# One decoder kernel: in its last attention, four heads' products in four groups of rows together, and one output tile a batch

## The reference

```
def _L1_xattn_ref(q, k, v, Wq, bq, Wk, bk, Wv, bv, Wo, bo):
    qh = (q @ Wq + bq).reshape(B, LQ, HEADS, D_K).transpose(0, 2, 1, 3)
    kh = (k @ Wk + bk).reshape(B, LKV, HEADS, D_K).transpose(0, 2, 1, 3)
    vh = (v @ Wv + bv).reshape(B, LKV, HEADS, D_K).transpose(0, 2, 1, 3)
    scores = jnp.einsum('bhqd,bhkd->bhqk', qh, kh) * scale
    attn = jax.nn.softmax(scores, axis=-1)
    out = jnp.einsum('bhqk,bhkd->bhqd', attn, vh)
    concat = out.transpose(0, 2, 1, 3).reshape(B, LQ, D_MODEL)
    return concat @ Wo + bo
```

## Time and profile before

| | |
|---|---|
| median of 3 runs | 792.78 us (789.83 to 793.07) |
| profiled execution, its own time | 796.1 us |
| its span | 794.3 us |
| busy: TensorE, VectorE, ScalarE, GpSimd | 719.1, 489.1, 412.9, 290.0 us |
| mean granted clock of TensorE | 0.937 of 2.4 GHz |

### The profile page before, as it was taken

The page is one execution under the profiler, slowest core; times in us unless marked ns, Lnnn a source line. Parts: engine busy times, 40 slices in busy tenths (PEclk is TensorE's granted clock), DMA queues, the critical chain, the costliest instruction groups (busy, mean ns, idle before and its releaser), DMA issues.

```text
span 794.3 us, 16402 instructions
## 1 busy us (share of the span) xinstructions
PE 719.1 (91%) x5852; PEld 542.2 (68%) x5852; DVE 489.1 (62%) x1297; ACT 412.9 (52%) x1047; POOL 290.0 (37%) x395
## 2 busy tenths in 40 slices
PE   8788889898897998999999989989888899999886
PEld 6565567575665765899898967758566455767665
DVE  4669777887977885444543455545455658583643
ACT  2234556657566677554544467555562545454311
POOL 0015355565555666110000036423350646363300
PEclk8869989999999999999999999999998756999999
DMA  8537451533727471000000000001011501000000
GB/s 235 126 69 179 123 128 43 122 83 88 161 46 205 112 214 57 2 1 1 1 1 1 1 1 4 1 2 41 4 38 54 185 26 31 2 2 9 8 7 7
DMA packets 25175, 48.11 MB, mean 61 GB/s; under 512 B 7264, under 2 KB 14192, under 8 KB 25096
## 3 DMA queue, kind: packets, MB, share of 16 engines
q1 hardware_dynamic: 24376, 45.66, 22.7%
q10 hardware_dynamic: 720, 1.41, 0.5%
HBM read 17.49 MB, written 0.52 MB: 23 GB/s over the span
## 4 chain that ended last, share of the span: by engine, by line
PE 60%; DVE 14%; issue 10%; ACT 8%; SPq 3%; POOL 2%; DMA 2%; POOLq 0%; ACTq 0%; DVEq 0%
PE SC L839 7%; PE G L550 7%; PE SC L826 7%; PE SC L769 5%; PE G L625 4%; PE SC L861 3%; PE G L938 3%; DVE shift_cols L1542 3%; PE SO L812 3%; ACT causal_probs L1154 2%; PE SO L893 2%; PE SC L743 2%; PE G L647 2%; SPq L1769 1%; PE G L577 1%
## 5 line engine op out<-in xcount | busy, mean ns | idle before, releaser
L1169 ACT ACTIVATE exps<-SC 128x512 f32<-128x512 f32 x192 | 114.4, 597 | 106.8 <-PE SC L769 106.1
L1542 DVE TENSOR_REDUCE shift_cols<-SC 128x2 f32<-128x512 f32 x192 | 129.5, 684 | 32.0 <-PE SC L743 31.5
L1621 POOL TENSOR_TENSOR rstd<-variance,consts 128x2 f32<-128x2 f32 (+1 forms) x48 | 36.8, 766 | 266.0 <-DVE variance L1234 263.0
L1689 POOL TENSOR_TENSOR VB<-exps 128x256 f32<-128x256 f32 x128 | 95.7, 756 | 59.4 <-ACT exps L1169 58.6
L1143 ACT ACTIVATE hidden<-SC,cols 128x256 f32<-128x256 f32 x128 | 53.6, 471 | 65.4 <-PE SC L826 65.3
L1711 POOL TENSOR_TENSOR causal_probs<-causal_probs,inverse 128x256 f32<-128x256 f32 x64 | 51.6, 828 | 68.9 <-DVE inverse L1555 68.9
L1576 DVE SCALAR_TENSOR_TENSOR R<-SC,small,R 128x128 f32<-128x128 f32 x128 | 39.0, 346 | 54.0 <-PE SC L839 53.3
L1154 ACT ACTIVATE causal_probs<-SC,negmax 128x128 f32<-128x128 f32 (+1 forms) x128 | 52.3, 424 | 37.1 <-DVE negmax L1550 37.0
L769 PE MATMUL SC<-stacked_q,stacked_k 100*128 100x256 f32 x256 | 66.9, 344 | 3.5 <-DMA stacked_q<-shift_rows 1.9
L839 PEld LDWEIGHTS SC<-ffn_w,hidden 128*128 128x128 f32 x512 | 66.0, 192 | 5.3 <-issue 1.8
L839 PE MATMUL SC<-ffn_w,hidden 128*128 128x128 f32 x512 | 67.6, 276 | 0.0
(11 more groups left out here) (257 smaller groups left out, 1504.5 us busy)
## 6 DMA issues: line engine op xcount, KB each, us to landing
stacked_k<-k_hi SPq DMA_DIRECT2D x64, 128.0 KB, 2.4
stacked_q<-q_hi SPq DMA_DIRECT2D x64, 128.0 KB, 2.4
ffn_w<-in_ffn_w SPq DMA_DIRECT2D x16, 512.0 KB, 4.8
stacked_k<-k_lo SPq DMA_DIRECT2D x32, 128.0 KB, 2.4
stacked_q<-q_lo SPq DMA_DIRECT2D x32, 128.0 KB, 2.5
packed_k<-U SPq DMA_DIRECT2D x48, 32.0 KB, 1.9
packed_q<-YN SPq DMA_DIRECT2D x48, 32.0 KB, 1.9
a_weights<-in_a_li SPq DMA_DIRECT2D x3, 256.0 KB, 7.4
```

Source lines behind the costliest of these rows:

```text
L1169: fn(exps[:, n % EXPS, :, :].rearrange("p t q -> p (t q)"), SC[1][:, n % 2, :, :].rearrange("p t q -> p (t q)"), ACT.Exp, scale=ATTENTIONS ...
L1542: v.tensor_reduce(shift_cols[:, n // UNIT % 4, :, n % UNIT], SC[0][:, n % 2, :, :], axis=AX.X, op=ALU.max, negate=True).then_inc(head_max, 1)
L1689: v.tensor_tensor(kept[n % EXPS].rearrange("p t q -> p (t q)"), exps[:, n % EXPS, 0, :], exps[:, n % EXPS, 1, :], ALU.add).then_inc(kept_r ...
```

## The change

- The products of the cross attention get a function of their own, `cross_products`: every second slot, at the front, for heads n and n+1 and, with a lag of 10 slots (CROSS_LAG), for the transposed products of heads n-10 and n-9. The eight matmuls go to the four groups of rows and to four banks, in turn. It waits for `head_max` of all heads before n and for `head_exp` of all before n-10.
- All 16 heads of a batch go into one bank: outputs in columns 0 to T, sums in columns T to 2T. The values of unit u have their 8 columns moved by 8 u in the 32, among zeros (`clear_values`, two clearings on GpSimd; `cross_values` writes in two parts), and the ones for the sums likewise (`own_rows`). The four units accumulate.
- ScalarE draws the sums, GpSimd checks, VectorE refines and divides once a batch (18, 18, 19 and 19 slots behind the last unit's first head), when all outputs have been written. The first unit of the next batch waits for the division.
- `project_out` has one chunk in place of four; `lx_wo` is 128 x 128. `mix(b)` begins one slot later (slot 16 b + 32).

The core of the diff:

```diff
-SHIFT_LAG = 9
+SHIFT_LAG, CROSS_LAG = 9, 10
+CROSS_INVERT, CROSS_REFINE, CROSS_DIVIDE = 18, 19, 19
+CROSS_OUT_AFTER = HEADS - UNIT + CROSS_DIVIDE + 1
...
 def mix_at(b):
-    return LX_AT + HEADS * b + OUT_AFTER
+    return LX_AT + HEADS * b + CROSS_OUT_AFTER
...
 def project_out(s, t):
...
-                    if at["d"] == HD:
+                    if s // NB == LX:
+                        c0, chunks = 4 * (s % 2), 1
+                        pe.wait_ge(cross_divided, CROSS_UNIT + s % NB + 1)
...
+                def cross_products(n, m):
+                    if n is not None:
+                        if n == STACK_HEADS:
+                            pe.wait_ge(exp_ready, NB * PAIRS)
+                            pe.wait_ge(key_ones_in, 16 * 2)
+                        pe.wait_ge(head_max, n)
+                        if n % UNIT == 0:
+                            pe.wait_ge(packed_in[n // UNIT % 4], 16 * 6 * (stream_of(n) % NB + 1))
+                    if m is not None:
+                        pe.wait_ge(head_exp, m)
+                        if m % UNIT == 0:
+                            pe.wait_ge(shifts_in[m // UNIT % 4], 16 * (m // UNIT // 4 + 1))
+                    for t in range(TT):
+                        of = slice(t * P, (t + 1) * P)
+                        if n is not None:
+                            for h in (n, n + 1):
+                                q, kk = packed(h, HD - 1)
+                                last = mm(SC[0][:, h % 2, t, :], q[:, of], kk, start=True, stop=True)
+                                if t == TT - 1:
+                                    last.then_inc(shift_scores, 1)
+                        if m is not None:
+                            for h in (m, m + 1):
+                                q, kk = packed(h, HD)
+                                last = mm(SC[1][:, h % 2, t, :], kk[:, of], q, start=True, stop=True)
+                                if t == TT - 1:
+                                    last.then_inc(head_scores, 1)
...
+                def cross_sum(U_):
+                    n, u = UNIT * U_, U_ % 4
+                    if u == 0:
+                        cross_place(stream_of(n) % NB)
+                    pe.wait_ge(kept_ready, n + UNIT)
+                    own = const("own_rows")[:, HD0 * (3 - u):HD0 * (3 - u) + HD]
+                    for k in range(UNIT):
+                        mm(SO[HD * k:HD * k + HD, T:2 * T], own, kept[(n + k) % EXPS].rearrange("p t q -> p (t q)"),
+                           start=u == 0, stop=False)
+                def cross_place(b):
+                    if b == 0:
+                        wait_emptied(pe, ("OC", 4 * NB - 1))
+                    else:
+                        pe.wait_ge(cross_divided, CROSS_UNIT + b)
+                def cross_unit_values(U_):
...
+                            last = mm(SO[HD * k:HD * k + HD, 0:T], cross_value(s, kt, h0 + k), exps[:, (n + k) % EXPS, kt, :],
+                                      start=False, stop=u == 3 and kt == TT - 1)
+                    last.then_inc(cross_outputs, 1)
...
+                def cross_sums_drawn(b):
...
+                    act.wait_ge(cross_outputs, CROSS_UNIT + 4 * (b + 1))
+                    fn(unit_sums[:, b % 2, :], SO[:, T:2 * T], ACT.Copy)
+                    fn(unit_inverse[:, b % 2, :], SO[:, T:2 * T], ACT.Ln).then_inc(cross_drawn, 1)
```

More of the change, by code:

```diff
@@ L122 @@
 LX_AT = L1_AT + NB * PAIRS
-LAST = LX_AT + HEADS * (NB - 1) + OUT_AFTER + 31
+LAST = LX_AT + HEADS * (NB - 1) + CROSS_OUT_AFTER + 31
 LINEAR_SLOTS = [
@@ L187, in head_of, with late_head @@
     return None
+def late_head(slot, more=0):
+    for lag, last in ((SHIFT_LAG, False), (CROSS_LAG, True)):
+        n = head_of(slot - lag - more)
+        if n is not None and (n >= STACK_HEADS) == last:
+            return n
+    return None
 def unit_of(slot, at):
@@ L193, in unit_of, with stacked_unit, cross_batch @@
     return n // UNIT if n is not None and n % UNIT == 0 else None
+def stacked_unit(slot, at):
+    U_ = unit_of(slot, at)
+    return U_ if U_ is not None and U_ < CROSS_UNIT else None
+def cross_batch(slot, at):
+    U_ = unit_of(slot, at)
+    return (U_ - CROSS_UNIT) // 4 if U_ is not None and U_ >= CROSS_UNIT and U_ % 4 == 3 else None
 def stream_of(n):
@@ L419, in decoder @@
         hidden_ready = sem("hidden_ready")
+        cross_outputs, cross_divided, cross_drawn = bank_filled["out"][0], bank_emptied["out"][0], bank_emptied["pair"][0]
         tile_number, tiles_of = {}, {r: 0 for r in RINGS}
@@ L972, in front @@
                 def front(slot):
-                    if head_of(slot) is not None:
-                        head_products(head_of(slot))
+                    n, m = head_of(slot), late_head(slot)
+                    if n is not None and n < STACK_HEADS:
+                        head_products(n)
+                    even = [h if h is not None and h >= STACK_HEADS and h % 2 == 0 else None for h in (n, m)]
+                    if even != [None, None]:
+                        cross_products(*even)
                     if unit_of(slot, TURN_AT) is not None:
@@ L1472, in cross_values @@
                     g = wait_filled(dve, ("v", s))
-                    v.tensor_tensor(VB[s % 2][:, 0:TT * C].rearrange("p (t c) -> p t c", c=C),
-                                    g[:, 0:TT * C].rearrange("p (t c) -> p t c", c=C), over_tiles(row("bv")), ALU.add)\
-                        .then_inc(*emptied(("v", s)))
+                    dve.wait_ge(packed_cleared, 4 + s % 2 + 1)
+                    if b >= 2:
+                        dve.wait_ge(cross_outputs, CROSS_UNIT + 4 * (b - 1))
+                    for t in range(TT):
+                        part = [x.rearrange("p (u k d) -> p u k d", u=4, k=UNIT)
+                                for x in (g[:, t * C:(t + 1) * C], row("bv"))]
+                        last = v.tensor_tensor(cross_values_of(s, t), part[0], part[1], ALU.add)
+                    last.then_inc(*emptied(("v", s)))
                     yield 1
```

160 lines of the change are left out of this document (104 added, 56 removed).

## The result

The changed kernel takes **808.7 us** (median of 4 executions, 797.9 to 817.4) against 792.9 (4 executions, 789.8 to 795.0): ratio **1.0128, 95% interval 1.0067 to 1.0189**. It is slower; the forecast was 785 us, range 769 to 799. The interval leaves out executions more than 1.5% above the fastest of the same kernel, and here that cuts off the upper part of one continuous spread, so the median shows more than the ratio.

The account below looks back on a forecast made before the run. The last attention was taken as mostly TensorE-bound, with VectorE full from 700.8 to 711.4. Terms by stage summed to -8.8 us, giving 784.0 against the median of 792.8; forecast 785 us, range 769 to 799.

Parts of the forecast that it names:

- Products together: Cross attention: eight matmuls cost what four did, saving TensorE 0.43 us (full clock) or 0.73 (half) per pair of slots.
- rival 3: Whole kernel: gain and waits cancel, also if eight matmuls are not as cheap at full clock; 790 to 792 us; chance 0.20.
- light stage: First transposed product to batch 0's slot tables, 612.6 to 674.1, 38 slots: sum -3.2 us, taken as -3.
- What that adds: Each group waits for both maxima and exponentials of the last: bare pair 1.9 us at full clock, four slots 4.2.
- The pair with a turn: Cross attention, pair whose slots include the turn's matmul and ScalarE's copy: 2.3 us at full clock, 2.9 at half.
- 592.8 to 612.6: Causal layer's rest beside the first scores: nine single products become five groups, -1.7 us, taken as -1.5.
- The stretches with `up1`: 677.9 to 700.8 and 713.8 to 736.3: savings of 3.1 us each, cancelled by 3.1 of waits; nothing left.
- 700.8 to 711.4 and 736.3 to 743.8: VectorE-bound stretches: fewer refinements and divisions, -1.5 us in the first and -1.3 in the second.
- From 743.8 on: End of the kernel: batch 3's output products leave TensorE's chain, -1.5 us.
- The tile: One tile a batch: 12 of 16 refinements and divisions, 12 draws and checks, three quarters of output products removed; 1.35 us a batch.
- The clock: Least certain term, 612.6 to 674.1: all at half clock some 65 us (+3.7), at full about 50 (-12).
- The second: Rival: each of 37 groups waits for the later of VectorE and ScalarE; at 0.35 us extra each, 797 us; chance 0.23.

Follow-up runs that it names:

- tile_only: The kernel before with only the one tile a batch; products single as before, lag 9; 799.0 us, ratio 1.0052.
- again: The changed kernel, unaltered, run and profiled once more; 811.4 us, ratio 1.0122.
- early: The changed kernel with both exponentials and both maxima of a pair moved to the front of the group's slot; 795.8 us, ratio 1.002.
- exps_early: The changed kernel with only ScalarE's two exponentials of a pair moved to the front, maxima one a slot; 808.1 us, ratio 1.0158.
- early_tight: The changed kernel with both exponentials and maxima moved to the front, and each batch's draws, guess, refinement and division one slot earlier; 801.5 us, ratio 1.0019.
- before_again: The kernel before, unaltered, with a profile of its own; 795.2 us, ratio 0.9999.
- after_warm: The changed kernel with three unused matmuls of zeros ahead of each group's wait in slots 10 to 46; 804.2 us, ratio 1.0097.
- tile_warm: One tile a batch with single products, plus two matmuls of zeros before each head's products in slots 10 to 46; 827.4 us, ratio 1.0409.

## Why the prediction was wrong, step by step

- **Products together.** Right: eight in 0.44 us at full (679.17 to 679.61) and 0.74 at half clock (645.29 to 646.03). The remark under rival 3 that no row at full clock shows eight together overlooked one in the trace of before: 707.95 to 708.40. In the light stage TensorE's work fell by 14.9 us; the forecast had 12 + 2.7.
- **What that adds: the step that failed.** I put 2.7 and 2.9 us on a pair at half clock and 4.2 on two pairs at full clock, and some 4 us besides on the steps in between. The groups of after at full clock:

```profile
624.01 0.38 PE L796 MATMUL SC<-packed_k,packed_q 31*128 31x256 f32 x2
...
626.33 0.39 PE L796 MATMUL SC<-packed_k,packed_q 31*128 31x256 f32 x2 [0.94 <-ACT exps L1284]
...
629.18 0.39 PE L796 MATMUL SC<-packed_k,packed_q 31*128 31x256 f32 x2 [0.71 <-DMA packed_q<-shift_rows]
```

The pair with a turn (624.01 to 626.33) took the 2.3 us forecast; at half clock such pairs took 2.8 (617.93 to 620.76), forecast 2.9. What failed is the other pair. It took 2.9 us at full clock (626.33 to 629.18) where the sum has 1.9, and with the projections 5.6 and 7.1 us (612.34 to 617.93, 638.20 to 645.29) where the terms give 2.7 + 1.0 = 3.7. These two pairs alone are 5.3 us over. I had priced the compact copies by their own length, and not by what the first of them waits for (the projection's product at the one place, a transfer at the other, though the earlier trace rows showed the queue of such transfers), and had left out VectorE's steps behind them, which stand before the second maximum. Idle time rose by 17.9 us where the sum has 11.5 (14.7 of saving less 3.2), that is 0.34 us too little at each of 19 groups. The stage came out at +3.0, not -3.
- **592.8 to 612.6.** Forecast -1.5, measured -1.0 (18.8 for 19.8), and that at a clock of 1.00 for 0.89.
- **The stretches with `up1`.** Right in sum. From batch 0's tokens to the first `up1`, 3.75 us before (674.15 to 677.90) and 5.32 now (674.29 to 679.61): forecast +1.1, measured +1.6; from there to the eighth slot 1.4 less (21.5 for 22.9).
- **700.8 to 711.4 and 736.3 to 743.8.** Wrong: -1.5 and -1.3 forecast, 10.6 became 10.9 and 7.5 became 7.4. VectorE's work did shrink (10.10 to 9.53), but TensorE's group at 711.32 now waits 1.65 us for a maximum behind the slot tables.
- **From 743.8 on.** -1.5 forecast, +1.3 measured (51.8 for 50.5), with a clock of 0.93 for 1.00 in the first half.
- **The tile.** The sum gives it most of its gain outside the light stage, and 2.7 us of output products inside. Its work went away as forecast, and at equal clock no time with it (tile_only: 793.7 at 0.94, before 793.8). Which of its terms failed is shown for one only: the -1.5 for batch 3's output products, since the stretch in which they stand, from the third to the fourth gathering of tokens, took 24.6 us in tile_only (738.5 to 763.1) as in before (743.8 to 768.4).
- **The clock.** I named it the least certain term and bounded it inside one stage, at +3.7. Two things were missing: in again that stage came out at 68.0 us with a clock of 0.58, and later stages, which the sum took at full clock, lost it in some executions (37.0 us at 0.83 for 31.9). What goes with the clock is two thirds of the difference between the means, and no term of the sum stands for it.

**The rivals.** The second, lock step dearer than the saving, is what happened, at nearly its price: it asked for 0.35 us a group above the forecast and gave 797 us; measured were 0.34 in the light stage and 798.8 at 0.94 (the median, 808.7, lies far above it, by the clock). It had a chance of 0.23 and should have had the most. I had argued that the odd slots' work covers a good part of the wait. It covers TensorE's own time; it does not bring the readers, which hold the steps of both slots in front of their second half. That this order makes the loss is what early shows, by moving only the order. What keeps the saving from coming out even then (15.7 us idle in early's light stage) was not taken apart.

The sentence of the Trainium skill (TensorEngine Tiling (Array Packing), Performance Considerations) that tiling does not speed up the emptying of PSUM agrees with the trace so far as TensorE's work fell by 14.9 us and none of it came out. But VectorE was busy for 35.4 and ScalarE for 24.6 of the 64.5 us: the readers were not full, their order held them. The 1.9 us that the forecast took for a pair by the emptying alone was not seen; the shortest pair without a turn took 2.8 (663.13 to 665.97).

**What stays open** is why the clock is lower. It may go with TensorE's waits in part: early, with 8.6 us of waits fewer and the same work, had 0.936, the changed kernel 0.919, exps_early 0.919. But early_tight, which differs from early in three constants, had 0.925, and tile_only, with TensorE as full as before, 0.932. Early_tight's light stage had a higher clock than early's (0.73 for 0.67) and its tail a lower one (0.74 for 0.90), and before_again has a tail at 0.75. The added work of after_warm raised the clock where it was put, and the tail had 0.62. No run separates these. None of the kernels beats the one before; early equals it.

## What to carry to other kernels

Grouping products so that one group fills every bank of a buffer buys TensorE time and sells the decoupling: in this kernel each group then waited for the last of all its readers, with whatever stands ahead of them in their queues. Before making such a change, write down for each reader what its queue holds between the group and its last operation, and price each entry by what it waits for, not by its own length; then move both readers' operations to the front: here moving ScalarE's alone was worth nothing, and moving both gave back the loss, though not a gain. Where an engine's work is taken away in a stage that others pace, expect idle time, and look at the granted clock of that stage and of those after it before counting on a gain.

## What the runs showed of the hardware that was not expected

- The same tail (some 156 matmuls, the same instructions) took 24.3 us at a granted clock of 0.97 (tile_only), 25.9 at 0.90 (before), 29.4 at 0.74 (again) and 33.6 at 0.62 (after_warm). The execution alone can do it: the unaltered kernel before had 25.9 at 0.90 and 29.5 at 0.75.
- The light stage ran at a mean clock of 0.67 while TensorE was busy for 57.0 of 61.5 us with products of 31 and 32 rows and outputs of 32 columns; in tile_warm, with matmuls of zeros of 128 rows among them, it had 0.84 (busy for 88.5 of 88.9; without them, in tile_only, 0.64).
- Eight products in four groups of rows take 0.44 to 0.45 us at full clock whether they are issued in turn over the groups or head by head.
- The mean clock of a whole execution of one unaltered kernel scatters from 0.922 to 0.952 (76 executions of before), and its time follows with 4.6 us per 0.01: more than the size of most edits tried here. Times of two kernels were comparable only beside their clocks.
